# K's blocks projected before Q's, a second plain pair of tiles in V's phase, and ffn rounding spread over an iteration

## The chip, the cores and the metric

The kernel runs on one core of one Trainium2 chip. The metric is the device time of one execution in microseconds (us). The kernel before takes 2241.61 us (median of 3 runs, 2234.49 to 2244.3).

## The reference, cut to what matters

x is (8, 512, 1024), every weight 1024 x 1024. There are 16 heads of 64.

```python
q, k, v = proj(x, Wq), proj(x, Wk), proj(x, Wv)      # y = x @ W.T, split into heads
q = q * min(cond, 4)[:, None]                        # one factor for each batch
scores = q @ k.T / sqrt(64), causal                  # 512 x 512 for each head
out = softmax(scores) @ v ; y = out @ Wo.T
alpha = max(mean(|Wf|), 1e-5)
q_w = clip(round(Wf / alpha), -1, 1) * alpha         # ternary weights
q_y = clip(round(y / s), -128, 127) * s              # s = absmax of the row / 127
result = x + q_y @ q_w.T + bias
```

## The kernel before, in words

Every fp32 operand is held as a high part (rounded to fp32r) and a low part (the remainder), and each product is three passes: low by high, high by low, high by high. ScalarE (ACT) writes the high part, VectorE (DVE) or GpSimd (POOL) subtracts it to give the low part. The order of the instructions on each engine is written out by hand. There are three phases.

**V's phase.** The 32 token tiles of 128 are taken as 16 pairs. The first pair is computed plainly (`v_plain`, L788, 96 matmuls of 128x512 into the four banks of `s_ps` and `proj_ps`). The other 15 go by a Strassen-Winograd scheme of seven half-size products (`v_product`, L803, 7 x 12 = 84 matmuls), which needs sums of blocks of Wv (`wv_sums`, L720, on DVE, then `ws_high`, L730, on ACT and `ws_low`, L736, on DVE) and sums of blocks of x (`xv_sums`, L773, on POOL). Results go through `v_high` (L875) and `v_low` (L884) into the two halves of `v_out`, each stored by `store_v` (L699) before it is used again. In the same phase the ffn weight is made ternary, one slice in each of eight iterations (`wf_ternary`, L919, three DVE operations in a chain, written at the end of the iteration), and the first x of the next phase is loaded (`load_x`, L342).

**Attention.** 4 groups of 4 heads by 8 batches are 32 steps. A step overlaps `old` (the previous batch) with `now`. In it TensorE (PE) does, for `now`, four projections into `proj_ps` in the order of `groups` (L152): block 0 of Q, block 0 of K, block 1 of Q, block 1 of K, each 8 slices of 3 matmuls (L174). A block is two heads. `J(gi, k)` in the step is slice k of projection gi, `S(u)` the scores of unit u (4 heads by 4 query tiles, 16 units), `T(u)` the transposes of its probabilities, `PV(h)` the product with V. The step of `now` reaches its own S(0) after J(2,5), and units 6 to 15, so S(8) too, come in the next step, where the batch is called `old`.

When a projection is ready, ACT writes its high parts (`evac_hi`, L194) and DVE its low parts (`evac_lo`, L212), two heads each. In the programs of ACT and DVE this is V(0) to V(2), and V(3) is the first thing of the next step. High and low parts of a head lie in opposite halves of the partitions, and the scores need K with its halves exchanged as well, `k_sw`. This copy is made by two DMAs on SP's queue:

```python
def swap_k(sp, it, blk):
    sp.wait_ge(proj_lo_done, it * NEV + EVAC[2 * blk + 1])
```

The first head of each block waits for it (`if u % (2 * QT) == 0: pe.wait_ge(k_swapped[h // 2], ...)`, L235), so S(0) waits for the exchange of K's block 0 and S(8) for that of block 1. SP's queue in a step is, in order: exchange of block 1 of `old`, `load_x` of the next batch, `load_v` 0 and 1, `store_o` 0 of `old` (L336), exchange of block 0 of `now`, `load_v` 2 and 3, `store_o` 1 of `old`. `store_o` 1 waits for `o_add` of head 3 (`OA(3)`, L333 on DVE). Q's evacuation takes a factor that `batch_scale` (L367) computes on DVE for the next batch, after Q's block 1 has been evacuated, behind V(2). One unit runs S on PE, mask and row minimum on DVE (L253), exponential on ACT (L260), reciprocal on DVE (L266), scaling on POOL (L272), T on PE (L282), high part on ACT (L296), low part `L(u)` on DVE (L303). T(u) waits for L(u - 2), whose bank it takes.

**The end.** The output projection (L508) and the ternary product (L579) run over 32 token tiles.

Of the kernel before, what the change touches and what calls it, by code (L numbers as in the profile page):

```python
# [11 lines left out]
P = 128  # L12
# [24 lines left out]
def adaln_ffn_kernel(nc, x, xT, cond, wq, wk, wv, wo, wf, bias, out):  # L37
# [4 lines left out]
    with ExitStack() as ctx:  # L42
# [83 lines left out]
        w_in = [sem(f"w{n}_in") for n in "qk"]  # L126
# [25 lines left out]
        groups = [("q", 0), ("k", 0), ("q", 1), ("k", 1)]  # L152
# [5 lines left out]
        def project(pe, it, g, gi, k):  # L158
            kind, n = groups[gi]
            bank = proj_ps[gi % 2]  # L160
            w = "qkv".index(kind)
# [64 lines left out]
        def swap_k(sp, it, blk):  # L226
            sp.wait_ge(proj_lo_done, it * NEV + EVAC[2 * blk + 1])
            heads = slice(2 * blk, 2 * blk + 2)
            sp.dma_start(k_sw[0:DH, heads, :].bitcast(F32), k_st[DH:P, heads, :].bitcast(F32)).then_inc(k_swapped[blk], 16)  # L229
            sp.dma_start(k_sw[DH:P, heads, :].bitcast(F32), k_st[0:DH, heads, :].bitcast(F32)).then_inc(k_swapped[blk], 16)  # L230

        def scores(pe, it, u):
            h, qt = divmod(u, QT)
            n = it * UNITS + u
            if u % (2 * QT) == 0:  # L235
                pe.wait_ge(k_swapped[h // 2], (it + 1) * 32)
            if due(count := n - 1):
                pe.wait_ge(max_done, count)
# [128 lines left out]
        def batch_scale(dve, it, b):  # L367
# [15 lines left out]
        def load_w(sp, g):  # L383
            if due(count := 4 * g):
                sp.wait_ge(wqk_lo_done, count)
            for n in range(2):
                sp.dma_start(w_raw[n][:, :, :], (wq, wk)[n][bass.ds(g, 1), :, :, :]
                             .rearrange("a p k e -> p (a k) e")).then_inc(w_in[n], 16)

        def split_w_qk(eng, it, g, gi, low):  # L390

            kind, blk = groups[gi]
            w = "qkv".index(kind)
# [5 lines left out]
            else:  # L399
                eng.wait_ge(w_in[w], (g + 1) * 16)  # L400
                if isinstance(it, int) and it < 0:
                    eng.wait_ge(v_product_done, V_LAST + (1 if kind == "q" else 2))
# [229 lines left out]
        V_LAST = 7 * (PAIRS - 2)  # L632
# [4 lines left out]
        B_PLAIN = [[T2, T1], [T3, T4]]  # L637
# [12 lines left out]
        xv_sum_done = sem("xv_sum_done")  # L650
        v_plain_done = sem("v_plain_done")
# [23 lines left out]
        def plain_bank(j, i):  # L675
            return (s_ps, proj_ps)[j][i]

        def load_xv(sp, n):
            if n == 2:
                sp.wait_ge(xv_lo_done, 4)  # L680
            elif n > 2:
                sp.wait_ge(xv_lo_done, 4 + 7 * (n - 2))
# [16 lines left out]
        def store_v(sp, n, q):  # L699
            j, i = V_RESULT_PLAIN[q] if n == 0 else V_RESULT[q][:2]  # L700
# [29 lines left out]
        def ws_high(act, c):  # L730
            act.wait_ge(wv_sum_done, WV_SUM_COUNT[c])
            if c == A21_PLAIN:
                act.wait_ge(v_plain_done, 4)
# [9 lines left out]
        def xv_split_plain(eng, i, j, low):  # L743
            c = B_PLAIN[i][j]
            n = 2 * i + j
            if low:
                eng.wait_ge(xv_hi_done, n + 1)
                eng.tensor_tensor(xv[:, c, 1, :], xv_quad(0, i, j), xv[:, c, 0, :].bitcast(F32),
                                  ALU.subtract).then_inc(xv_lo_done, 1)
            else:  # L750
                eng.wait_ge(xv_first_in[i], 32)
                eng.activation(xv[:, c, 0, :], xv_quad(0, i, j), ACT.Copy).then_inc(xv_hi_done, 1)

        def xv_split(eng, n, c, low):
            if n >= PAIRS:
                return
            count = 4 + 7 * (n - 1) + c
# [7 lines left out]
            if n > 1:  # L765
                eng.wait_ge(v_product_done, 7 * (n - 2) + c + 1)
            elif c == T2:
                eng.wait_ge(v_plain_done, 4)
            if c >= T2:
                eng.wait_ge(xv_sum_done, 4 * (n - 1) + {T1: 1, T3: 2, T2: 3, T4: 4}[c])  # L770
            eng.activation(xv[:, c, 0, :], xv_quad(n, *XV_PLACE[c]), ACT.Copy).then_inc(xv_hi_done, 1)

        def xv_sums(pool, n):  # L773
# [3 lines left out]
            base, done = 4 + 7 * (n - 1), 4 * (n - 1)  # L777
# [9 lines left out]

        def v_plain(pe):  # L788
            for k in range(KT):
# [3 lines left out]
                ks = slice(k % CH * P, (k % CH + 1) * P)  # L793
                for j in range(2):
                    c = B_PLAIN[k // CH][j]
                    for i, a in enumerate((A11, A21_PLAIN) if k < CH else (A12, A22)):
                        for m, (xp, wp) in enumerate(((1, 0), (0, 1), (0, 0))):
                            mm = pe.matmul(plain_bank(j, i)[:, :], xv[:, c, xp, ks], wv_view(a, wp)[:, k % CH, :],
                                           start=(k == 0 and m == 0), stop=(k == KT - 1 and m == 2))
                        if k == KT - 1:  # L800
                            mm.then_inc(v_plain_done, 1)

        def v_product(pe, n, c):  # L803
            done = 4 * (n - 1)
            pe.wait_ge(xv_lo_done, 4 + 7 * (n - 1) + c + 1)
            if n == 1 and c in ws_lo_done:
                pe.wait_ge(ws_lo_done[c], 1)
            if c == A11:
                bank = bank_x[n % 2]
                if due(count := done - 4):  # L810
                    pe.wait_ge(v_sum_done, count)
            elif c == S4:
                bank = bank_w
                if due(count := done - 1):
                    pe.wait_ge(v_sum_done, count)
            elif c == A12:
                bank = bank_z
                if due(done):
# [21 lines left out]
        def v_copy(act, n, which):  # L840

            c, bank = [(A11, bank_x[n % 2]), (S2, bank_x[n % 2]), (S1, bank_z), (A22, bank_z)][which]
            act.wait_ge(v_product_done, 7 * (n - 1) + c + 1)
            if n > 1:
# [3 lines left out]
        def v_sum(dve, n, q):  # L848
            place = V_RESULT[q][2]
            if q == 0:  # L850
                bank = bank_z
                dve.wait_ge(v_product_done, 7 * (n - 1) + A12 + 1)
                dve.wait_ge(v_copy_done, 4 * (n - 1) + 1)
            elif q == 1:
                bank = bank_x[n % 2]
                dve.wait_ge(v_product_done, 7 * (n - 1) + S3 + 1)
                dve.wait_ge(v_ur_done, n)
            elif q == 2:
                bank = bank_w
# [11 lines left out]
        def v_source(n, q):  # L871
            src = plain_bank(*V_RESULT_PLAIN[q])[:, :] if n == 0 else v_tmp[:, V_RESULT[q][2], :]
            return src.rearrange("p (h d) -> p h d", d=DH)

        def v_high(act, n, q):  # L875
            if n == 0:
                act.wait_ge(v_plain_done, q + 1)
            else:
                act.wait_ge(v_sum_done, 4 * (n - 1) + q + 1)
# [12 lines left out]
        WF_ABS_FROM, WF_FROM = 2, 6  # L892
# [26 lines left out]
        def wf_ternary(dve, k):  # L919
            raw = wf_tmp[k % 2]  # L920
            dve.wait_ge(wf_in[k % 2], ((KT + k) // 2 + 1) * 16)
            if k >= 2:
                dve.wait_ge(wf_stored[k % 2], k // 2 * 16)
            dve.tensor_scalar(raw, raw, alpha[:, 1:2], MAGIC, ALU.mult, ALU.add).then_inc(wf_chain, 1)
            dve.wait_ge(wf_chain, 4 + 2 * k)
            dve.tensor_scalar(raw, raw, MAGIC, 1.0, ALU.subtract, ALU.min).then_inc(wf_chain, 1)
            dve.wait_ge(wf_chain, 5 + 2 * k)
            dve.tensor_scalar(wf_out[k % 2], raw, -1.0, None, ALU.max).then_inc(wf_q_done, 1)
# [9 lines left out]
        def v_sp(sp):  # L938
# [10 lines left out]
            for n in range(1, PAIRS):  # L949
# [4 lines left out]
                if n == 1:  # L954
# [13 lines left out]
                if n == WF_FROM + KT:  # L968
                    for slot in wf_stored:
                        sp.wait_ge(slot, KT // 2 * 16)  # L970
                    load_x(sp, 0, 0)

        def v_pe(pe):
            v_plain(pe)
            for n in range(1, PAIRS):
# [10 lines left out]
        def v_act(act):  # L986
            load_wv(act, 0)
            for i, (k0, k1) in enumerate(V_PIECES):
                if i == 0:
                    xv_split_plain(act, 0, 0, False)  # L990
                    xv_split_plain(act, 0, 1, False)
                if i == 2:
                    xv_split_plain(act, 1, 0, False)
                    xv_split_plain(act, 1, 1, False)
# [9 lines left out]
            xv_split(act, 1, T2, False)  # L1004
            xv_split(act, 1, T1, False)
            ws_high(act, S3)
            xv_split(act, 1, T3, False)
            xv_split(act, 1, T4, False)
            for q in range(4):
                v_high(act, 0, q)  # L1010
            for n in range(1, PAIRS):
# [638 lines left out]
```

## Time and profile before

| | |
|---|---|
| median of 3 runs | 2241.61 us |
| the profiled execution's own time | 2243.83 us |
| its span | 2241.8 us |
| mean granted TensorE clock | 0.975 |
| PE busy | 2033.3 us, 91% |
| DVE busy | 1422.6 us, 63% |
| ACT busy | 1119.2 us, 50% |
| POOL busy | 898.7 us, 40% |

The page of the profile divides the span into the busy time of the engines, the chain of work that ended last, and groups of instructions with the idle time ahead of them. A group's idle time is put down to what ended it. Answers of the trace used below are: who waited for whom, the instructions in order of time, and the busy time and granted clock of a stretch. V's phase runs to 341.6 us, attention to about 1760, and the end from there.

### The profile page before, as it was taken

To read this page: it belongs to the slowest core of one execution; us is meant where nothing else is said; L and a number is where in the kernel's file an instruction comes from. 1 tells how busy PE (TensorE), PEld (TensorE's weight loads), DVE (VectorE), ACT (ScalarE), POOL (GpSimd) and SP (SyncE) were. 2 spreads that over 40 slices of the span, in tenths; PEclk is the share of its full clock that TensorE was granted. 3 is DMA by queue.
4 is the path that set the end of the run, shared out by engine and by line. 5 is a ranking of instruction groups with operands and counts; after the bars stand their busy time and mean duration, and the time that the engine had idled before them with its cause. 6 is when DMAs were issued, how large, how long until landed. Compare 5 with 4: busy or idle time off the path is not lost.

```text
span 2241.8 us, 34702 instructions
## 1 busy us (share of the span) xinstructions
PE 2033.3 (91%) x10031; PEld 1640.5 (73%) x10062; DVE 1422.6 (63%) x3284; ACT 1119.2 (50%) x2504; POOL 898.7 (40%) x821
## 2 busy tenths in 40 slices
PE   6999998898989898898989888898988899999998
PEld 4778886776777777777767777777776677777776
DVE  7657775666667666667666667666666655445544
ACT  4454454666657666666666666666666300000000
POOL 2443333434334433434443343344334444444442
PEclk9999999999999999999999999999999999999999
DMA  5766644323343433343343334334235423333332
GB/s 150 239 221 211 209 178 148 104 90 119 117 134 94 131 103 98 103 163 105 95 131 103 98 103 165 104 94 140 94 98 158 134 95 102 112 112 95 102 112 75
DMA packets 200980, 282.42 MB, mean 126 GB/s; under 512 B 11216, under 2 KB 146384, under 8 KB 199760
## 3 DMA queue, kind: packets, MB, share of 16 engines
q1 hardware_dynamic: 200384, 281.07, 39.3%
q8 instruction: 33, 0.54, 0.1%
q10 hardware_dynamic: 528, 0.52, 0.1%
q14 instruction: 35, 0.29, 0.0%
HBM read 178.79 MB, written 69.21 MB: 111 GB/s over the span
## 4 chain that ended last, share of the span: by engine, by line
PE 69%; DMA 12%; DVE 9%; issue 4%; ACT 4%; SPq 2%; DVEq 0%; ACTq 0%
PE proj_ps L174 20%; DMA k_sw<-k_st 11%; PE s_ps L508 8%; PE proj_ps L508 7%; PE t_ps L835 7%; PE o_ps L316 7%; PE o_ps L835 5%; PE o_ps L579 5%; PE t_ps L282 4%; DVE k_st L223 4%; PE s_ps L241 3%; PE s_ps L242 2%; SPq L229 1%; DVE parts L364 1%; ACT pt_hi L296 1%
## 5 line engine op out<-in xcount | busy, mean ns | idle before, releaser
L174 PE MATMUL proj_ps<-parts 128*128 128x512 f32 x3072 | 858.3, 414 | 0.0
L272 POOL TENSOR_TENSOR prob<-prob,row_inv 128x128 f32<-128x128 f32 (+3 forms) x512 | 386.1, 754 | 846.3 <-DVE row_inv L266 843.9
L174 PEld LDWEIGHTS proj_ps<-parts 128*128 128x128 f32 x3072 | 550.1, 193 | 98.6
L260 ACT ACTIVATE prob<-prob,row_min 128x128 f32<-128x128 f32 (+3 forms) x512 | 287.2, 561 | 160.0 <-DVE row_min L253 155.5
L253 DVE CUSTOM_DVE_ANT_0 prob<-s_ps,mask 128x128 f32<-128x128 f32 (+3 forms) x512 | 248.3, 485 | 119.4 <-PE s_ps L242 54.9
L296 ACT ACTIVATE pt_hi<-t_ps 128x128 fp32r<-128x128 f32 (+3 forms) x512 | 221.9, 433 | 194.4 <-PE t_ps L282 189.1
L282 PE MATMUL t_ps<-ident,prob 128*128 128x128 f32 x1280 | 229.4, 277 | 52.8 <-DVE pt_lo L303 50.4
L303 DVE TENSOR_TENSOR pt_lo<-t_ps,pt_hi 128x128 fp32r<-128x128 f32 (+3 forms) x512 | 249.5, 487 | 31.0 <-ACT pt_hi L296 20.7
L241 PE MATMUL s_ps<-k_sw,q_st 128*128 128x128 f32 (+3 forms) x512 | 164.7, 322 | 114.9 <-DMA k_sw<-k_st 114.8
L564 ACT ACTIVATE yt_q<-t_ps 128x1024 bf16<-128x1024 bf16 x32 | 32.8, 1024 | 426.6 <-PE t_ps L557 426.6
L241 PEld LDWEIGHTS s_ps<-k_sw,q_st 128*128 128x128 f32 x512 | 96.8, 189 | 160.6 <-issue 108.9
L282 PEld LDWEIGHTS t_ps<-ident,prob 128*128 128x128 f32 x1280 | 152.5, 141 | 77.2 <-DVE pt_lo L303 46.9
L364 POOL TENSOR_TENSOR parts<-x_raw,parts 128x512 fp32r<-128x512 f32 x128 | 194.6, 1521 | 16.0 <-ACT parts L358 16.0
L333 DVE TENSOR_TENSOR o_sum<-o_ps,o_low 64x512 f32<-64x512 f32 x128 | 87.5, 683 | 172.4 <-ACT o_low L325 172.3
L508 PE MATMUL proj_ps<-parts,o_parts 128*128 128x512 f32 x768 | 188.2, 400 | 4.0 <-POOL o_parts L486 4.0
L508 PE MATMUL s_ps<-parts,o_parts 128*128 128x512 f32 x768 | 185.1, 396 | 0.0
L316 PE MATMUL o_ps<-pt_lo,v_st 128*128 128x512 f32 (+3 forms) x512 | 171.7, 345 | 2.6 <-DVE pt_lo L303 2.6
L508 PEld LDWEIGHTS proj_ps<-parts,o_parts 128*128 128x128 f32 x768 | 143.9, 190 | 35.1 <-POOL o_parts L486 4.2
L242 PE MATMUL s_ps<-k_st,q_st 128*128 128x128 f32 (+3 forms) x512 | 166.1, 324 | 0.0
L508 PEld LDWEIGHTS s_ps<-parts,o_parts 128*128 128x128 f32 x768 | 142.8, 188 | 30.6
L316 PE MATMUL o_ps<-pt_hi,v_st 128*128 128x512 f32 (+3 forms) x512 | 157.5, 343 | 0.0
L266 DVE RECIPROCAL row_inv<-row_sum 128x1 f32<-128x1 f32 x512 | 82.3, 161 | 102.0 <-ACT prob L260 98.7
(106 smaller groups left out, 2968.3 us busy)
## 6 DMA issues: line engine op xcount, KB each, us to landing
x_raw<-xT SPq DMA_DIRECT2D x128, 512.0 KB, 5.5
v_scratch<-v_out SPq DMA_DIRECT2D x64, 512.0 KB, 3.3
k_sw<-k_st SPq DMA_DIRECT2D x128, 256.0 KB, 3.7
v_st<-v_scratch SPq DMA_DIRECT2D x128, 256.0 KB, 2.7
oT_scratch<-o_sum SPq DMA_DIRECT2D x64, 256.0 KB, 2.1
x_raw<-oT_scratch SPq DMA_DIRECT2D x32, 512.0 KB, 4.8
x_tile<-x SPq DMA_DIRECT2D x32, 512.0 KB, 5.4
out<-res SPq DMA_DIRECT2D x32, 512.0 KB, 3.2
```

The costliest lines, as they stand in the source:

```text
L174: mm = pe.matmul(out, l, r, start=(k == 0 and i == 0), stop=(k == KT - 1 and i == 2))
L241: pe.matmul(s_ps[u % 2][:, 0:w], q, k_sw[:, h, 0:w], start=True, stop=False)
L253: dve.tensor_tensor_reduce(prob[:, u % 4, 0:w], s_ps[u % 2][:, 0:w], mask[:, S - w:S], 1.0, -MASKED, ALU.add, ALU.min, row_min[:, u % 4:u ...
L260: act.activation(prob[:, u % 4, 0:w], prob[:, u % 4, 0:w], ACT.Exp, bias=row_min[:, u % 4:u % 4 + 1], scale=-1.0, accum_out=row_sum[:, u % ...
L272: pool.tensor_tensor(prob[:, u % 4, 0:w], prob[:, u % 4, 0:w], row_inv[:, u % 4:u % 4 + 1].broadcast_to([P, w]), ALU.mult).then_inc(norm_d ...
L282: mm = pe.transpose(t_ps[u % 2][:, kb * P:(kb + 1) * P], prob[:, u % 4, kb * P:(kb + 1) * P], ident[:, :])
L296: act.activation(pt_view(pt_hi[h % 2], qt), t_ps[u % 2][:, 0:(qt + 1) * P] .rearrange("p (k q) -> p k q", q=P), ACT.Copy).then_inc(pt_hi_d ...
L303: dve.tensor_tensor(pt_view(pt_lo[h % 2], qt), t_ps[u % 2][:, 0:(qt + 1) * P] .rearrange("p (k q) -> p k q", q=P), pt_view(pt_hi[h % 2], q ...
L316: mm = pe.matmul(o_ps[h % 2][:, q0:S], v, part[h % 2][:, kb, q0:S], start=(kb == 0 and part is pt_lo), stop=(kb == QT - 1 and part is pt_hi))
L364: eng.tensor_tensor(x_lo[:, k, :], x_raw[:, k, :], x_hi[:, k, :].bitcast(F32), ALU.subtract).then_inc(x_lo_done[k % 2], 1)
L508: mm = pe.matmul(y_ps[p][half][:, :], a[p][:, o], b[k][:, w], start=(k == 0 and i == 0), stop=(k == KT - 1 and i == 2))
L835: mm = pe.matmul(bank[:, :], xv[:, c, xp, ks], wv_view(c, wp)[:, k, :], start=(k == 0 and m == 0 and c not in (S2, S3)), stop=(k == CH - 1 ...
```

## The change

Three parts. **Groups:** the order becomes K 0, Q 0, K 1, Q 1. The exchange of a block of K waits for K's evacuation (V(0), V(2)), which is one projection earlier; PE gets a wait for Q's evacuation at S(0) and S(8). On SP the exchange of `now`'s block 0 moves ahead of `load_v` 1 and `store_o` 0. `batch_scale` moves from behind V(2) to behind V(3), where Q's block 1 is evacuated now. The weights' buffers, loads and splits change places accordingly. **V's phase:** the second pair is plain as well, into the banks of `o_ps` and `t_ps`; fourteen pairs are left for the seven products. **ffn:** the three operations of the rounding are issued at three places of an iteration, the whole of that work runs one iteration later (from 7 instead of 6), and `load_x` waits for its last store at the start of the last iteration.

```diff
-        groups = [("q", 0), ("k", 0), ("q", 1), ("k", 1)]
+        groups = [("k", 0), ("q", 0), ("k", 1), ("q", 1)]
@@ swap_k
-            sp.wait_ge(proj_lo_done, it * NEV + EVAC[2 * blk + 1])
+            sp.wait_ge(proj_lo_done, it * NEV + EVAC[2 * blk])
@@ scores
                 pe.wait_ge(k_swapped[h // 2], (it + 1) * 32)
+                pe.wait_ge(proj_lo_done, it * NEV + EVAC[h // 2 * 2 + 1])
@@ batch_scale
-                if due(count := (it - 1) * NEV + EVAC[2]):
+                if due(count := (it - 1) * NEV + EVAC[3]):
@@ dve_step
             if old:
                 evac_lo(dve, o, 3)
+                if now:
+                    batch_scale(dve, n, now[2])
...
             V(2)
-            if nxt:
-                batch_scale(dve, *nxt)
@@ sp_step
             if now and old:
                 load_v(sp, *now, 0)
+            if now:
+                swap_k(sp, now[0], 0)
+            if now and old:
                 load_v(sp, *now, 1)
...
                 store_o(sp, *old, 0)
-            if now:
-                swap_k(sp, now[0], 0)
@@ V's phase
+        PLAIN = 2
-        B_PLAIN = [[T2, T1], [T3, T4]]
+        B_PLAIN = [[[T2, T1], [T3, T4]], [[B11, B21], [B22, T2]]]
+        PLAIN_BANKS = [s_ps + proj_ps, [bank_x[0], bank_w, bank_z, bank_x[1]]]
@@ v_plain, behind the first pair
+            for j in range(2):
+                pe.wait_ge(xv_lo_done, 4 + 2 * j + 2)
+                for i in range(2):
+                    for k in range(KT):
+                        mm = v_plain_slice(pe, 1, j, i, k)
+                    mm.then_inc(v_plain_done, 1)
@@ v_act, behind the splits of Wv
-            xv_split(act, 1, B11, False)
-            xv_split(act, 1, B22, False)
-            xv_split(act, 1, B21, False)
+            xv_split_plain(act, 1, 0, 0, False)
+            xv_split_plain(act, 1, 1, 0, False)
+            xv_split_plain(act, 1, 0, 1, False)
+            xv_split_plain(act, 1, 1, 1, False)
+            for q in range(4):
+                v_high(act, 0, q)
             ws_high(act, S4)
             ws_high(act, S2)
             ws_high(act, S1)
+            xv_split(act, 2, B11, False)
+            xv_split(act, 2, B22, False)
+            for q in range(2):
+                v_high(act, 1, q)
+            xv_split(act, 2, B21, False)
...
@@ v_dve
+                if n == WF_FROM:
+                    wf_scale(dve)
+                wf_ternary(dve, n - WF_FROM, 0)
...
                 v_low(dve, n, 0)
+                wf_ternary(dve, n - WF_FROM, 1)
...
                 xv_split(dve, n + 1, T1, True)
+                wf_ternary(dve, n - WF_FROM, 2)
...
-                if WF_FROM <= n < WF_FROM + KT:
-                    wf_ternary(dve, n - WF_FROM)
@@ v_sp
+                if n == PAIRS - 1:
+                    for slot in wf_stored:
+                        sp.wait_ge(slot, KT // 2 * 16)
+                    load_x(sp, 0, 0)
                 for q in range(4):
                     store_v(sp, n, q)
...
-                if n == WF_FROM + KT:
-                    for slot in wf_stored:
-                        sp.wait_ge(slot, KT // 2 * 16)
-                    load_x(sp, 0, 0)
```

## Rows read from the trace of the kernel before

**Rows 1.** The page: shares of the chain that ended last, by line.
```profile
PE proj_ps L174 20%; DMA k_sw<-k_st 11%; PE s_ps L508 8%; PE proj_ps L508 7%; PE t_ps L835 7%; PE o_ps L316 7%; PE o_ps L835 5%; PE o_ps L579 5%; PE t_ps L282 4%; DVE k_st L223 4%; PE s_ps L241 3%; PE s_ps L242 2%; SPq L229 1%; DVE parts L364 1%; ACT pt_hi L296 1%
```

**Rows 2.** Who waited for whom: us in total, times, longest.
```profile
PE s_ps L241 <- DMA k_sw<-k_st: 114.8, 63, 6.3
...
PE t_ps L282 <- DVE pt_lo L303: 50.4, 37, 1.7
```

**Rows 3.** Busy us and granted clock (PEclk, DMA share, GB/s last) of five stretches.
```profile
34.68:71.56 36.88, 24.05 (x85) 18.90 (x84) 27.57 (x26) 18.43 (x24) 7.48 (x5) 0.77 0.30 100
...
71.56:90.60 19.04, 19.04 (x85) 15.77 (x84) 11.00 (x15) 8.15 (x14) 7.25 (x5) 1.00 0.90 314
...
406.19:1716.63 1310.44, 1158.62 (x6000) 966.99 (x6000) 869.60 (x2442) 856.64 (x2052) 535.68 (x601) 0.97 0.36 115
...
1127.57:1150.51 22.94, 21.52 (x106) 18.03 (x107) 13.01 (x38) 12.38 (x30) 6.40 (x9) 0.93 0.45 148
...
1215.37:1236.72 21.35, 19.96 (x106) 16.79 (x107) 13.02 (x38) 12.37 (x30) 6.39 (x9) 1.00 0.48 158
```

**Rows 4.** PE in order of time, V's opening: start, us, instruction, idle before.
```profile
43.03 7.19 PE L835 MATMUL t_ps<-wv_first,xv 128*128 128x512 f32 x23 [5.47 <-DVE wv_first L738]
...
57.81 5.46 PE L835 MATMUL o_ps<-wv_first,xv 128*128 128x512 f32 x12 [7.36 <-ACT v_tmp L846]
```

**Rows 5.** DVE and ACT in order of time, V's opening.
```profile
36.32 2.29 DVE L728 TENSOR_TENSOR wv_raw<-wv_raw 128x2048 f32<-128x2048 f32 x1
...
38.65 3.71 ACT L734 ACTIVATE wv_first<-wv_raw 128x2048 fp32r<-128x2048 f32 x2 [14.22 <-DVE wv_raw L728]
...
55.28 0.60 ACT L882 ACTIVATE v_out<-proj_ps 128x512 fp32r<-128x512 f32 x1 [6.27 <-DMA v_scratch<-v_out]
```

**Rows 6.** PE in order of time, one step: S(0), T(4), S(8), the next S(0).
```profile
1062.76 0.33 PE L241 MATMUL s_ps<-k_sw,q_st 128*128 128x128 f32 x1 [1.31 <-DMA k_sw<-k_st]
...
1079.75 0.33 PE L282 MATMUL t_ps<-ident,prob 128*128 128x128 f32 x1 [1.27 <-DVE pt_lo L303]
...
1083.68 0.32 PE L241 MATMUL s_ps<-k_sw,q_st 128*128 128x128 f32 x1 [2.21 <-DMA k_sw<-k_st]
...
1106.62 0.32 PE L241 MATMUL s_ps<-k_sw,q_st 128*128 128x128 f32 x1 [1.44 <-DMA k_sw<-k_st]
```

**Rows 7.** DVE in order of time, the same step: V(2), batch_scale, OA(3), V(3), L(3).
```profile
1067.44 1.53 DVE L219 SCALAR_TENSOR_TENSOR q_st<-proj_ps,q_scale,q_st 64x512 fp32r<-64x512 f32 x2 [0.34 <-ACT q_st L204]
1069.01 0.15 DVE L374 TENSOR_SCALAR q_scale<-cond_bc 128x1 f32<-128x1 f32 x1
...
1075.69 0.68 DVE L333 TENSOR_TENSOR o_sum<-o_ps,o_low 64x512 f32<-64x512 f32 x1 [0.46 <-ACT o_low L325]
...
1077.70 1.41 DVE L223 TENSOR_TENSOR k_st<-proj_ps,k_st 64x512 fp32r<-64x512 f32 x2
...
1080.93 0.68 DVE L303 TENSOR_TENSOR pt_lo<-t_ps,pt_hi 128x512 fp32r<-128x512 f32 x1
```

**Rows 8.** SP's queue in order of time, the same step: store_o 1, exchange of block 1.
```profile
1076.45 0.36 SPq L340 DMA_DIRECT2D oT_scratch<-o_sum  x1
...
1079.65 0.59 SPq L230 DMA_DIRECT2D k_sw<-k_st  x1
```

**Rows 9.** Time from issue to landing: the exchanges (tile k_sw), and the page's DMA issues.
```profile
DMA to landing us min/median/max: 3.0/3.7/7.6
...
oT_scratch<-o_sum SPq DMA_DIRECT2D x64, 256.0 KB, 2.1
...
wf_scratch<-x_raw SPq DMA_DIRECT2D x8, 256.0 KB, 2.3
```

**Rows 10.** From V's phase into attention: SP, ACT, and a piece of the chain.
```profile
326.87 2.20 SPq L348 DMA_DIRECT2D x_raw<-xT  x4
...
338.05 0.58 ACT L846 ACTIVATE v_tmp<-t_ps 128x512 f32<-128x512 f32 x1
...
355.34 7.60 DMA k_sw<-k_st
```

More of the change, by code:

```diff
@@ L786, in xv_sums, with v_plain_slice @@
             pool.tensor_tensor(b21, b21, b22, ALU.subtract).then_inc(xv_sum_done, 1)
+        def v_plain_slice(pe, p, j, i, k):
+            c, a = B_PLAIN[p][k // CH][j], (A11, A21_PLAIN, A12, A22)[2 * (k // CH) + i]
+            ks = slice(k % CH * P, (k % CH + 1) * P)
+            for m, (xp, wp) in enumerate(((1, 0), (0, 1), (0, 0))):
+                mm = pe.matmul(PLAIN_BANKS[p][2 * j + i][:, :], xv[:, c, xp, ks], wv_view(a, wp)[:, k % CH, :],
+                               start=(k == 0 and m == 0), stop=(k == KT - 1 and m == 2))
+            return mm
         def v_plain(pe):
@@ L792, in v_plain @@
                     pe.wait_ge(xv_lo_done, 2 * (k // CH) + 2)
-                ks = slice(k % CH * P, (k % CH + 1) * P)
                 for j in range(2):
[L795 to L799, printed above, removed]
+                    for i in range(2):
+                        mm = v_plain_slice(pe, 0, j, i, k)
                         if k == KT - 1:
                             mm.then_inc(v_plain_done, 1)
+                if k == CH - 1:
+                    mm.then_inc(v_half_done, 1)
+            for j in range(2):
+                pe.wait_ge(xv_lo_done, 4 + 2 * j + 2)
+                for i in range(2):
+                    for k in range(KT):
+                        mm = v_plain_slice(pe, 1, j, i, k)
+                    mm.then_inc(v_plain_done, 1)
         def v_product(pe, n, c):
-            done = 4 * (n - 1)
-            pe.wait_ge(xv_lo_done, 4 + 7 * (n - 1) + c + 1)
-            if n == 1 and c in ws_lo_done:
+            done = v_first(n)
+            pe.wait_ge(xv_lo_done, xv_count(n) + c + 1)
+            if n == PLAIN and c in ws_lo_done:
                 pe.wait_ge(ws_lo_done[c], 1)
@@ L967, in v_sp @@
                         load_wf(sp, KT + k + 2)
[L968 to L971 removed]
         def v_pe(pe):
             v_plain(pe)
[L975 removed]
+            for n in range(PLAIN, PAIRS):
                 v_product(pe, n, A11)
@@ L1003, in v_act @@
             ws_high(act, S1)
-            xv_split(act, 1, T2, False)
-            xv_split(act, 1, T1, False)
-            ws_high(act, S3)
[L1007 to L1011, printed above, removed]
+            xv_split(act, 2, B11, False)
[3 more added lines that the diff above has]
+            xv_split(act, 2, B21, False)
+            xv_split(act, 2, T2, False)
+            v_high(act, 1, 2)
+            xv_split(act, 2, T1, False)
+            ws_high(act, S3)
+            v_high(act, 1, 3)
+            xv_split(act, 2, T3, False)
+            xv_split(act, 2, T4, False)
+            for n in range(PLAIN, PAIRS):
                 v_copy(act, n, V_TMP_A)
@@ L1088, in v_dve @@
                 v_low(dve, n, 3)
-                if n == WF_FROM:
-                    wf_scale(dve)
-                if WF_FROM <= n < WF_FROM + KT:
-                    wf_ternary(dve, n - WF_FROM)
         def v_pool(pool):
-            xv_sums(pool, 1)
-            for n in range(1, PAIRS):
+            xv_sums(pool, PLAIN)
+            for n in range(PLAIN, PAIRS):
                 xv_sums(pool, n + 1)
```

182 lines of the change are left out of this document (107 added, 75 removed).

## The prediction

> **What bounds the kernel now.** I read the page's chain first. Behind the projections (20%) its largest item is no engine but a transfer: the exchange of K's halves, 11% of the span [rows 1]. The list of waits says what of that PE feels: S(0) and S(8) wait for it 63 times, 114.8 us in all [rows 2]. PE's only other large wait in attention is for the low parts of the probabilities, 50.4 us. Then the instructions of one step in order of time: S(8) at 1083.68 waits 2.21 us, S(0) at 1106.62 waits 1.44 [rows 6]. Of the 63, one is the first S(0) (6.34 us by its row, 6.3 here); the 31 others at S(0) are 1.31 to 1.44 us, say 1.39, together 43.1; what is left, 114.8 - 6.3 - 43.1 = 65.4 us, is 31 waits at S(8), 2.11 each.
>
> The stretches show a second cost. S(8) to S(0) takes 21.35 us at a granted clock of 1.00 and 22.94 us at 0.93, the same work [rows 3]: after the waits at T(4) (1.27 us) and S(8) PE runs for a while at 1.2 instead of 2.4 GHz. 22 of the 31 such stretches are slow ones, so 22 x 1.57 = 34.5 us hang on PE's idling there. After S(0)'s single 1.4 us the clock does not fall.
>
> In V's phase PE is full (19.04 busy of 19.04 us for a pair [rows 3]) but for its opening: pair 1 takes from 34.68 to 71.56, 36.88 us, PE busy 24.05 at a clock of 0.77. It waits 5.47 us for the sums of Wv and 7.36 us for ACT, which sits 6.27 us waiting for a store of `v_out` before it may copy a bank [rows 4, 5].
>
> **V's opening.** The new plain pair is 96 matmuls where the old product had 84. A product's matmul is 19.04/84 = 0.2267 us at the full clock, so the pair costs 96 x 0.2267 = 21.76 us in place of 36.88: 15.1 us less, if nothing waits. Its splits of x come where the old ones came, ahead of the sums of Wv. The sums and splits of Wv now have the pair as cover: the sums end at 38.6 or sooner [rows 5], ACT is held by `v_high` of pair 0 (two of them wait for a store) until 41 to 44, then three `ws_high` of 1.85 us (half of 3.71 [rows 5]) and three `ws_low` on DVE of 2.3 us, a sum's time [rows 5], end at 49.5 to 52.5, and PE reaches the first product at 56.5. ACT must then pass two splits, `v_high` 1/2 and 1/3, a split, the last `ws_high` and two more splits, some 6.5 us, before the copy that frees pair 2's third accumulation, which PE reaches 8.2 us later: a slack of 1.7 us; DVE's first sum has under 1 us. Bounds for what is late next: 0 and 3 us. I take 0.3, since both slacks are above zero; without this cover the old stalls of 5.47 and 7.36 us come back. **-14.8 us.** The other 14 pairs do not change.
>
> **ffn rounding.** Three DVE operations of 0.7 us leave the end of an iteration. PE waits for nothing of theirs there (full at 1.00), and at the new places the splits of x run an iteration ahead: 0, bounds -0.5 and +1. But one thing moves with it: the last store of that work is now issued at about 327 and `load_x`, behind it on SP, waits for its landing, 2.3 us [rows 9], where it was issued at 326.87 [rows 10]. ACT's eight splits of x stand ahead of the copy at 338.05, which PE's last product waits for with no slack (it starts 0.15 us late already). x_high waited for no DMA before, so the cover is somewhere between 0 and 2.4 us: +0 to +2.4, I take **+1.3**.
>
> **S(0).** K 0 is evacuated at V(0), a projection of 24 matmuls and more before V(1), so at least 5.4 us sooner, and its exchange is issued then. On SP it stands behind `load_v` 0, which waits for PV(0), done before V(0); `load_v` 1 and `store_o` 0 behind it wait for PV(1) and later work, so nothing queued there is held. It lands 3.7 us on, well before S(0). The new wait is for Q 0's low parts at V(1), where the exchange began until now; an exchange takes 0.5 + 3.7 us, of which PE waits 1.4, so PE arrives 2.8 us after V(1). Behind the wait stand only T(13) and PV(2), ready by then. DVE's row minimum follows S(0) at once and its reciprocal before it ends 0.3 us ahead. **31 x 1.39 = -43.1 us.** The first S(0): four loads of x go ahead of the exchange on SP at 350.4, so it is issued at about 352.5 instead of 355.3 and its 7.6 us [rows 10] still show: **-2.5**.
>
> **S(8).** K 1 is evacuated at V(2), but the exchange stands on SP behind `store_o` 1, which waits for OA(3). Counted from S(0) at 1062.76 [rows 6]: OA(3) ends 13.6; the store takes SP 0.4, the exchange's halves 0.5 each, so the second is issued at 14.6 instead of 16.9 [rows 7, 8]; with 3.7 to 3.9 us it lands at 18.3 to 18.5. PE reaches S(8) at 20.92 - 2.21 = 18.7. On DVE, V(3) is Q's now: 1.53 instead of 1.41, and `batch_scale` 0.15 with its wait [rows 7], so L(2), T(4) and S(8) come 0.25 later, at 19.0; the low part L(3), which T(5) right behind S(8) needs, ends at 18.85 + 0.25 = 19.1, about when T(5) would go. V(2) is cheaper by as much, but DVE idles behind it anyway, so I give nothing for that. The store before the exchange lands 2.1 us after its issue [rows 9] and may delay it by up to 0.9. So of 2.11 us between 0.25 and 1.3 stay; by the nearest numbers (DVE's 0.25 and a little of the other) I take 0.35. **31 x 1.76 = -54.5 us.** `load_x` behind the exchange still waits for the last split of x, as before.
>
> **Clock.** With 1.5 to 1.9 us of idling at T(4) and S(8) in place of 3.4, more than after S(0) and less than now, the fall should go in most steps. Bounds 0 and -34.5; I take **-28**.
>
> Sum: -14.8 + 1.3 - 2.5 - 43.1 - 54.5 - 28 = -141.6 us, against the profiled execution's 2243.8: 2102. That execution is 2.2 us over the median of the runs shown, less than their spread of 9.8, so I leave it. As a check, attention's period is 1310.44/30 = 43.7 us [rows 3], and would be 43.7 - 1.39 - 1.76 - 0.9 = 39.6, with PE busy some 37.9 of it.
>
> **Rivals.**
>
> (a) The clock stays. PE's small waits go on (T(4) alone 1.27 us), and the stretches from S(8) may stay slow: 2102 + 28 = 2130. For it: 22 of 31 stretches fall now; against it: no stretch falls after S(0), whose wait is nearly as long as what will be left at S(8). The Trainium skill ("TensorE: Matmul & The Clock Gate", section "A second HAM failure mode: psum-queue depth-cycling") says that frequent micro-idles between groups of matmuls are enough to make the clock swing between its two levels; by that rule this rival would be the forecast.
>
> (b) The exchange of block 1 is as late as ever. If it and the store ahead of it share the engines fully, it lands 2.1 us later, at 20.5, against 20.9 now: S(8) gains 0.4 instead of 1.76, and the clock falls as before. 2102 + 31 x 1.36 + 28 = 2172. For it: two transfers on one queue within 0.5 us. Against it: the store's bytes are half of the exchange's, and it has landed by 15.8.
>
> (c) Slower. The same place, with the price that the trace shows when an exchange runs beside big loads: 7.6 us [rows 9, 10]. Behind the moved exchange comes `load_x`, four loads. Landing at 14.6 + 7.6 = 22.2 makes S(8) 1.3 us later than now, which eats S(0)'s 1.39; the clock would fall in the 9 other stretches too (+14), V's phase keeps its 13.5 and the first step 2.5: about 2239. Each further microsecond costs 31: from 8.1 us of landing on the kernel is over 0.5% slower, and at 8.5 it takes 2239 + 31 x 0.9 = 2267. Against it: `load_x` waits for the last split of x and is issued at 1082.4, 4.8 us after the moved exchange. The Trainium skill ("DMA: Bandwidth & Descriptors", section "Issuing engines are not separate DMA queues") says that all DMAs interleave on the same 16 engines, which is what makes this rival possible and says nothing of its size.
>
> (d) The change doesn't do what it says in attention, since Q's evacuation, now last, takes the place of the exchange. At S(0) it is done 2.8 us ahead; V(3) ends at 1079.1, 2.4 us ahead of PE at S(8) [rows 6, 7]. Nothing speaks for it; with only V's part left it would take about 2230.
>
> **Chances.** Forecast 0.64, (a) 0.18, (b) 0.10, (c) 0.03, (d) 0.02, and 0.03 for something under 2080. The forecast's own range is 2083 (all of the clock back and no residue: -14.8 - 2.5 - 43.1 - 65.4 - 34.5 = -160, and nothing lost at V's end) to 2120. With (a) and part of (b), and 1.0 us more at S(8) in a case between, the range is 2080 to 2150. 0.5% is 11 us, about what a measurement of this kernel tells from no change. Faster than that: all but (c) and a share of (d), 0.95; the same 0.03; slower 0.02.
>
> **What would show it.** PE's wait for `k_sw` under 25 us in total, and none at S(0) but the first; S(0) to S(0) near 39.6 us; the granted clock of S(8) to S(0) at 1.00; plain pair 1 at 34.7 to 56.5 with no wait over 0.5 us behind it; the last product of V's phase 1 to 2 us behind the one before. A sum of waits for `k_sw` over 60 us is rival (b); a clock of 0.93 with short waits is (a). The forecast is wrong as a whole if PE's waits for `pt_lo` (50.4 us now) grow past 80: then DVE, not the exchange, set S(8).

## The result

The changed kernel takes 2085.72 us (median of 4 runs, 2083.93 to 2087.4) against 2241.44 before: a ratio of 0.9309 (95% interval 0.9287 to 0.9332), 156 us less. It lies in the range given; the forecast was 2102.

The page of the changed kernel, its span, busy times and the chain by line (for [rows 1]); its own time is 2085.09 us at a mean clock of 0.994:

```profile
span 2083.3 us, 34749 instructions
...
PE 1991.5 (96%) x10074; PEld 1617.8 (78%) x10074; DVE 1416.1 (68%) x3277; ACT 1114.4 (53%) x2497; POOL 888.4 (43%) x816
...
PE proj_ps L174 24%; PE proj_ps L509 8%; PE s_ps L509 8%; PE o_ps L317 6%; PE o_ps L580 5%; PE t_ps L870 5%; PE t_ps L283 5%; PE o_ps L870 3%; PE s_ps L243 2%; PE s_ps L242 2%; DVE q_st L219 2%; ACT parts L359 2%; DVE prob L254 2%; DVE parts L365 1%; ACT prob L261 1%
```

The exchange, 11% of the chain before, is no longer among its lines. What PE still waits for most, from the list of waits (for [rows 2]; us, waits, the longest):

```profile
PE t_ps L283 <- DVE pt_lo L304: 50.8, 35, 2.8
```

and who waited for the tile `k_sw`, from the view of that tile:

```profile
  PE s_ps L242: 1.6, 2
```

Besides these two waits (0.45 us at one S(8), 1.14 us at one S(0)) the first S(0) waits 4.85 us. The list puts that down to "issue", but it is the exchange too: it was issued at 342.79, took 10.1 us to land, and S(0) starts at 352.97. So 114.8 us of waiting for the exchange, 6.3 of them at the first S(0), have become 6.5. The wait for `pt_lo` has not grown.

Five stretches (for [rows 3]): the new plain pair, the first pair of seven products, all 31 periods from S(0) to S(0), and the two parts of one step, S(0) to S(8) and S(8) to S(0):

```profile
34.00:55.76 21.76, 21.76 (x98) 18.03 (x96) 12.72 (x12) 8.62 (x9) 4.20 (x3) 1.00 0.56 193
55.76:74.80 19.04, 19.04 (x86) 15.77 (x84) 15.94 (x18) 11.81 (x20) 9.61 (x6) 1.00 0.43 139
...
352.97:1556.34 1203.37, 1151.61 (x6176) 973.49 (x6177) 893.59 (x2517) 881.59 (x2114) 552.17 (x619) 1.00 0.42 129
...
1130.57:1149.34 18.77, 17.33 (x96) 14.40 (x94) 14.54 (x40) 15.86 (x38) 10.58 (x11) 1.00 0.24 70
1149.34:1169.13 19.79, 19.79 (x107) 16.96 (x108) 13.82 (x43) 12.33 (x31) 7.18 (x10) 1.00 0.54 172
```

A period, from one S(0) to the next, is 1203.37/31 = 38.82 us where it was (1716.63 - 363.08)/31 = 43.66; the first and last S(0) before stood at 363.08 and 1716.63. From S(8) to S(0) PE is busy without a gap, at the full clock. Between the two profiled executions the span's 158.5 us come from: 8.6 until attention's first matmul (341.62 to 332.99), 1.5 from there to the first S(0), 150.2 in the 31 periods, and 1.8 back in the end.

PE, DVE and SP in order of time in that step (for [rows 6 to 8]): T(4), S(8) and the next S(0); OA(3), V(3), batch_scale, L(3); store_o 1, the exchange of block 1 behind it, load_x, the exchange of block 0.

```profile
1147.57 0.33 PE L283 MATMUL t_ps<-ident,prob 128*128 128x128 f32 x1 [1.41 <-DVE pt_lo L304]
...
1149.33 0.32 PE L242 MATMUL s_ps<-k_sw,q_st 128*128 128x128 f32 x1
...
1169.13 0.22 PE L242 MATMUL s_ps<-k_sw,q_st 128*128 128x128 f32 x1
```

```profile
1143.09 0.69 DVE L334 TENSOR_TENSOR o_sum<-o_ps,o_low 64x512 f32<-64x512 f32 x1 [0.45 <-ACT o_low L326]
...
1145.11 1.53 DVE L219 SCALAR_TENSOR_TENSOR q_st<-proj_ps,q_scale,q_st 64x512 fp32r<-64x512 f32 x2
1146.78 0.15 DVE L375 TENSOR_SCALAR q_scale<-cond_bc 128x1 f32 x1
...
1148.75 0.68 DVE L304 TENSOR_TENSOR pt_lo<-t_ps,pt_hi 128x512 fp32r<-128x512 f32 x1
```

```profile
1143.99 0.37 SPq L341 DMA_DIRECT2D oT_scratch<-o_sum  x1
1144.89 0.47 SPq L229 DMA_DIRECT2D k_sw<-k_st  x1
1145.41 0.59 SPq L230 DMA_DIRECT2D k_sw<-k_st  x1
1150.21 1.90 SPq L349 DMA_DIRECT2D x_raw<-xT  x4
...
1156.79 0.48 SPq L229 DMA_DIRECT2D k_sw<-k_st  x1
```

Two places gave less than was forecast. PE's last product of V's phase, then the first S(0) (for [rows 10]; the columns are start, us, instruction, idle before it):

```profile
328.67 4.48 PE L870 MATMUL t_ps<-wv_last,xv 128*128 128x512 f32 x12 [2.84 <-ACT v_tmp L881]
...
352.97 0.45 PE L242 MATMUL s_ps<-k_sw,q_st 128*128 128x128 f32 x1 [4.85 <-issue]
```

and ACT ahead of that product, where the splits of x wait for their loads, which stand on SP behind the landing of the last ffn store:

```profile
322.43 2.43 ACT L359 ACTIVATE parts<-x_raw 128x512 fp32r<-128x512 f32 x4 [1.40 <-DMA x_raw<-xT]
325.66 2.38 ACT L359 ACTIVATE parts<-x_raw 128x512 fp32r<-128x512 f32 x4 [0.80 <-DMA x_raw<-xT]
327.94 0.58 ACT L881 ACTIVATE v_tmp<-t_ps 128x512 f32<-128x512 f32 x1
```

### The profile page after: what moved, and what is told of

Same layout as the page of the kernel before. It is cut to its first block, busy times and chain, and to the rows that moved or that the text cites. A ratio compares the mean times of both kernels' runs of the same rounds, so it can differ in the third digit from the quotient of the medians.

```text
span 2083.3 us, 34749 instructions
## 1 busy us (share of the span) xinstructions
PE 1991.5 (96%) x10074; PEld 1617.8 (78%) x10074; DVE 1416.1 (68%) x3277; ACT 1114.4 (53%) x2497; POOL 888.4 (43%) x816
## 4 chain that ended last, share of the span: by engine, by line
PE 72%; DVE 10%; issue 6%; ACT 6%; DMA 3%; POOL 1%; DVEq 0%; SPq 0%; ACTq 0%; POOLq 0%
PE proj_ps L174 24%; PE proj_ps L509 8%; PE s_ps L509 8%; PE o_ps L317 6%; PE o_ps L580 5%; PE t_ps L870 5%; PE t_ps L283 5%; PE o_ps L870 3%; PE s_ps L243 2%; PE s_ps L242 2%; DVE q_st L219 2%; ACT parts L359 2%; DVE prob L254 2%; DVE parts L365 1%; ACT prob L261 1%
## 5 line engine op out<-in xcount | busy, mean ns | idle before, releaser
L174 PE MATMUL proj_ps<-parts 128*128 128x512 f32 x3072 | 840.9, 408 | 0.0
L174 PEld LDWEIGHTS proj_ps<-parts 128*128 128x128 f32 x3072 | 540.6, 190 | 95.8
L283 PE MATMUL t_ps<-ident,prob 128*128 128x128 f32 x1280 | 228.2, 277 | 53.1 <-DVE pt_lo L304 50.8
L242 PE MATMUL s_ps<-k_sw,q_st 128*128 128x128 f32 (+3 forms) x512 | 160.3, 313 | 7.5 <-issue 5.0
L317 PE MATMUL o_ps<-pt_lo,v_st 128*128 128x512 f32 (+3 forms) x512 | 161.2, 326 | 2.7 <-DVE pt_lo L304 2.7
L359 ACT ACTIVATE parts<-x_raw 128x512 fp32r<-128x512 f32 x256 | 146.0, 618 | 3.1 <-DMA x_raw<-xT 2.2
L317 PE MATMUL o_ps<-pt_hi,v_st 128*128 128x512 f32 (+3 forms) x512 | 147.0, 324 | 0.0
```

The source lines that it names most:

```text
L174: mm = pe.matmul(out, l, r, start=(k == 0 and i == 0), stop=(k == KT - 1 and i == 2))
L242: pe.matmul(s_ps[u % 2][:, 0:w], q, k_sw[:, h, 0:w], start=True, stop=False)
L283: mm = pe.transpose(t_ps[u % 2][:, kb * P:(kb + 1) * P], prob[:, u % 4, kb * P:(kb + 1) * P], ident[:, :])
L317: mm = pe.matmul(o_ps[h % 2][:, q0:S], v, part[h % 2][:, kb, q0:S], start=(kb == 0 and part is pt_lo), stop=(kb == QT - 1 and part is pt_hi))
```

## The experiments

All ratios are to the kernel before, timed beside it on the same chip.

**The change in two.** `groups_only` is the kernel before with the edits of `groups`, `swap_k`, `scores`, `batch_scale` and SP's order; `v_only` is the changed kernel with these undone.

> The kernel before with the attention part of the change alone (order K 0, Q 0, K 1, Q 1, the exchange's place on SP, batch_scale's place). Theory: the step of the changed kernel, 38.82 us instead of 43.66, comes wholly from this part: 31 x 4.84 = 150 us and 1.5 us at the first S(0), so 2090 us. Rival 1: the terms as I forecast them (1.39 + 1.76 a step and 28 of the clock): 2113. Rival 2: part of the step's gain needs V's phase (it starts attention in another state): above 2100 as well, with the clock below 0.99.

Measured: 2094.37 us, 0.9329 (0.9315 to 0.9343). Its mean period is 38.74 us. The theory holds for the step: the attention part alone gives 150 us, at a step that owes nothing to V's phase. Its 1.5 us at the first S(0) did not come: S(0) starts at 363.70 us, against 363.08 before, after a wait of 7.16.

> The kernel before with V's phase and the ffn rounding of the change, attention as it was. Theory: pair 1 takes 21.76 us instead of 36.88 (-15.1), V's end loses 2.8 us of waiting and 1.6 us of slow clock, and three small waits in the middle lose 2.3: -8.4, so 2233 us, with the step unchanged at 43.7. Rival (the late load of x shows only with the new order of the groups): -13, 2228.

Measured: 2232.68 us, 0.9949 (0.9935 to 0.9963), 11.5 us less. The interval, 8 to 15 us less, holds the theory's 8.4 and the rival's 13, so the trace has to tell. In order of time on PE: the last product has the same kind of wait ahead of it, 3.53 us; attention's first matmul starts at 335.59 us, 6.0 sooner than before and 2.6 later than in the changed kernel; and the first S(0) waits 2.70 us where it waited 6.34 before:

```profile
330.34 5.46 PE L869 MATMUL t_ps<-wv_last,xv 128*128 128x512 f32 x12 [3.53 <-ACT v_tmp L880]
335.59 9.71 PE L174 MATMUL proj_ps<-parts 128*128 128x512 f32 x40
...
353.90 0.44 PE L241 MATMUL s_ps<-k_sw,q_st 128*128 128x128 f32 x1 [2.70 <-DMA k_sw<-k_st]
```

So the late load of x is V's own, against the rival. The first S(0) comes 9.2 us sooner than before, near the theory's 8.4, but only 6.0 of them are there at attention's start; the other 3.2 come with the shorter wait, which the theory did not have. The mean period is 43.43 us, with 21 slow stretches from S(8) instead of 22.

**One block at a time.**

```diff
# block0_only (on the kernel before)
-        groups = [("q", 0), ("k", 0), ("q", 1), ("k", 1)]
+        groups = [("k", 0), ("q", 0), ("q", 1), ("k", 1)]
# block1_only (on the kernel before, with batch_scale behind V(3))
+        groups = [("q", 0), ("k", 0), ("k", 1), ("q", 1)]
```

Each exchange waits for its own block, and `scores` for the other operand where that is evacuated later.

> The kernel before with the order K 0, Q 0, Q 1, K 1: only block 0 is exchanged a projection sooner. Theory (the clock falls because of the waits at T(4) and S(8) together): S(0)'s wait of 1.39 us goes 31 times, S(8) keeps its 2.1 us and the stretches after it stay at a granted clock of 0.93: 2241 - 43 - 2 = 2197 us. Rival (the clock falls with the idle time of a step as a whole): the clock comes back too, 34 us more: 2162.

Measured: 2171.23 us, 0.967 (0.9655 to 0.9685). That is between the two and nearer to the rival (2162) than to the theory (2197). The waits are as the theory has them, 64.7 us over 31 at S(8), and none at S(0) but the first (6.2 us):

```profile
PE s_ps L242 <- DMA k_sw<-k_st: 64.7, 31, 2.4
```

but only 9 of the 31 stretches from S(8) to S(0) are slow, not 22 as before. The same stretch at both clocks:

```profile
425.46:446.79 21.33, 21.32 (x107) 18.25 (x107) 12.73 (x37) 11.51 (x29) 5.57 (x8) 0.92 0.48 157
467.76:487.56 19.80, 19.80 (x107) 16.97 (x107) 12.75 (x37) 11.52 (x29) 5.55 (x8) 1.00 0.51 170
```

Taking away S(0)'s wait, 20 us earlier in the step, prevented 13 of the clock's falls, worth 13 x 1.5 = 20 us. My reason for the falls, "after the waits at T(4) and S(8)", is half of it. How a wait so much earlier bears on them, no run shows.

> The kernel before with the order Q 0, K 0, K 1, Q 1: only block 1 is exchanged a projection sooner, and batch_scale moves. Theory: S(8)'s 2.11 us go and with them the clock's fall (34.5 us), S(0) keeps its 1.39: 2241 - 66 - 34 = 2140 us, granted clock 1.00 from S(8) to S(0). Rival (PE's small waits keep the clock low): 2175 us at a clock of 0.97.

Measured: 2144.67 us, 0.955 (0.9536 to 0.9565), near the theory. S(0) waits 1.3 to 1.6 us each time but the first, as in this row of PE in order of time:

```profile
688.32 0.33 PE L242 MATMUL s_ps<-k_sw,q_st 128*128 128x128 f32 x1 [1.30 <-DMA k_sw<-k_st]
```

Yet no stretch is slow; 400 us from the middle of attention, whose clock is the column of 1.00:

```profile
800.00:1200.00 400.00, 370.02 (x1981) 309.90 (x1980) 287.41 (x806) 283.78 (x678) 177.01 (x199) 1.00 0.39 123
```

The periods fall by 2.32 and 3.28 us, 174 us for both in 31 steps where the two together give 150: each alone brings back most of the clock (13 and 22 of the 22 falls), and it comes back once.

**What the queue's order is worth: rival (c).** `load_x` ahead of the exchange of block 1 in `sp_step`.

```diff
-            if old:
-                swap_k(sp, old[0], 1)
             if nxt:
                 load_x(sp, *nxt)
+            if old:
+                swap_k(sp, old[0], 1)
```

> The changed kernel with load_x ahead of the exchange of block 1 on SP, to price rival (c) of the prediction. The exchange is issued about 22 us after S(0) instead of 14.6 and runs beside four loads of 512 KB. Theory (transfers issued together share the engines): it lands 7 to 11 us after its issue, S(8) is 10 to 14 us later, 310 to 430 us in all, with the clock down in every step: 2400 to 2550 us. Rival (an exchange takes 3.7 us whatever runs beside it): S(8) is 6.5 us later, 2290 to 2330 us.

Measured: 2524.7 us, 1.1263 (1.1232 to 1.1293), at a mean clock of 0.914. The loads, the exchange, and PE at S(8), in one step:

```profile
1015.05 1.89 SPq L349 DMA_DIRECT2D x_raw<-xT  x4
1017.10 0.56 SPq L229 DMA_DIRECT2D k_sw<-k_st  x1
1017.70 0.61 SPq L230 DMA_DIRECT2D k_sw<-k_st  x1
```

```profile
1027.00 0.47 PE L242 MATMUL s_ps<-k_sw,q_st 128*128 128x128 f32 x1 [12.82 <-DMA k_sw<-k_st]
```

1027.0 - 1017.7 = 9.3 us from issue to use, where an exchange alone takes 3.7; over the 30 steps the second half lands 8.3 to 9.5 us after its issue. The theory holds, and rival (c)'s price is real. At S(8) its place is not in the changed kernel, where `load_x` is issued 4.8 us behind the exchange (1150.21 and 1145.41 above). But the same collision is there for block 0, whose exchange moved ahead of `load_v` 1. The view of the tile `k_sw` of the changed kernel:

```profile
DMA to landing us min/median/max: 3.1/3.7/13.2
```

In three steps, the first of each later group, this exchange is issued behind `load_x`, the loads of both weights and `load_v` 0, and lands after 10.4 to 13.2 us. S(0) comes late enough that PE waited for it only once, 1.14 us.

**V's end and the first step.**

```diff
# wf_store_early
                 for q in range(4):
                     store_v(sp, n, q)
+                    if q == 0 and WF_FROM <= n < WF_FROM + KT:
+                        store_wf(sp, n - WF_FROM)
...
-                    store_wf(sp, k)
# first_exchange: in the first step only, ahead of load_x
+            if now and not old:
+                swap_k(sp, now[0], 0)
...
-            if now:
+            if now and old:
                 swap_k(sp, now[0], 0)
```

> The changed kernel with the store of a rounded slice of the ffn weight issued behind the first of an iteration's four stores of V instead of behind the fourth. Theory: load_x no longer waits for that store's landing, PE's last product in V's phase loses its wait of 2.84 us and the slow clock behind it (1.6 us): -4.4, 2081 us. Rival (the loads of x themselves are the late ones, since they start after the fourth store of V either way): -1 or less.

Measured: 2082.88 us, 0.9289 (0.927 to 0.9307). `load_x` is issued 2.1 us sooner and PE's last product waits 0.4 us instead of 2.8, as the theory has it:

```profile
316.11 3.23 SPq L349 DMA_DIRECT2D x_raw<-xT  x4
```

In time the gain is 0.2% of the kernel, and its interval meets that of the changed kernel; the wait is shown, its 4 us are not. In the trace attention starts at 331.00 us. That is 2.0 sooner than in the changed kernel's profiled execution, which was a short one (see `first_exchange` below), and 4.9 to 6.3 sooner than in four others with its V's phase. The first S(0) gains less, 0.5 us against the changed kernel, since it now waits 6.39 us for the exchange instead of 4.85: the two edits of this section act on one path.

> The changed kernel with the exchange of block 0 ahead of load_x on SP in the first step only. Theory: the first S(0) waits 4.85 us because the exchange runs behind four loads of x; ahead of them it takes 3.7 us, the wait goes and with it the slow clock of some 3 us after it: -7 us, 2079. Rival (Q 0's evacuation is as late): -1 or less.

Measured: 2080.71 us, 0.9279 (0.926 to 0.9298). The wait at the first S(0) is gone, and the first step is 36.29 us long instead of 38.05. From attention's start to the first S(0) it is 15.0 us instead of 20.0, so with the step's 1.8 the size in the trace is the expected one; the interval overlaps with the changed kernel's by its edge.

This trace shows something more, since its V's phase is the changed kernel's, instruction for instruction. Yet attention starts at 335.89 us, not 332.99. PE waits 3.4 us for the sum of the ffn weight at 159 us in both, and behind that wait the clock was 1.00 in the changed kernel's profiled execution and 0.89 here:

```profile
158.00:190.00 32.00, 30.63 (x136) 25.41 (x137) 22.83 (x29) 14.31 (x27) 12.99 (x9) 1.00 0.65 203
...
158.00:190.00 32.00, 31.44 (x127) 25.86 (x128) 20.59 (x27) 12.93 (x24) 11.19 (x9) 0.89 0.58 186
```

It is 0.89 in `l2_first`, `l2_free` and `load_x_first` too, whose V's phase is also the same; attention starts at 336.4 to 337.3 there. So the profiled execution of the changed kernel was the lucky one of five: in the others V's phase ends 2.9 to 4.4 us later.

**The ffn rounding.** The three parts together at the end of an iteration again, in `v_dve`.

> The changed kernel with the three operations of the ffn rounding together at the end of an iteration again, at its new iterations. Theory (PE never waited for their place; what they set is when the last store, and behind it load_x, is issued): no other wait of PE in V's phase changes, the last rounding ends some 5 us later than in three parts, so load_x is issued 2 to 4 us later and V's end loses that: 2085 + 3 = 2088 us. Rival (three parts shorten waits in the middle of V's phase): three waits of PE of 0.6 to 1 us more in every iteration from 7 on, 2093 or more.

Measured: 2089.62 us, 0.9315 (0.9287 to 0.9344): no difference that the measurement tells. PE's waits in V's phase are the last product's, 3.7 us instead of 2.8, and 1.1 us at two others, so the rival's new waits are not there. `load_x` is issued 2.9 us later than in the changed kernel's profiled execution. But `first_exchange`, whose rounding is in three parts, has it as late. Its row of SP in order of time, behind that of `ffn_together`:

```profile
321.17 1.76 SPq L349 DMA_DIRECT2D x_raw<-xT  x4
...
321.05 1.76 SPq L349 DMA_DIRECT2D x_raw<-xT  x4
```

So the delay is not shown to come from the edit, and what the three places are worth, if anything, stays open.

**What is late next.** T(4) waits 1.41 us in each step for L(2), which stands behind V(3).

```diff
# l2_first, on DVE (and H(2) ahead of evac_hi on ACT)
+            L(2)
             if old:
                 evac_lo(dve, o, 3)
                 if now:
                     batch_scale(dve, n, now[2])
-            L(2)
# l2_free, besides: the exchange as soon as V(2) is done, ahead of store_o 1
-            if old:
+            if ending:
                 swap_k(sp, old[0], 1)
...
+            if now and not last:
+                swap_k(sp, now[0], 1)
             if old:
                 store_o(sp, *old, 1)
# l2_free_x6, besides (with wf_store_early and first_exchange):
# DVE's split of slice 6 from behind M(6) to behind L(4) and I(7)
```

> The changed kernel with the high and low parts of unit 2 (H(2) on ACT, L(2) on DVE) ahead of the evacuation V(3) instead of behind it, to price what is late now: T(4)'s wait for pt_lo, 1.41 us a step. Theory (DVE's order at the start of a step sets T(4), and V(3) has slack until S(8)): the wait goes, T(5)'s need of L(3) gives 0.2 back, 31 x 1.2 = 37 us less: 2086 - 37 = 2049 us. Rival (V(3) or the exchange becomes the last to arrive at S(8) at once, since its slack is no larger than what PE gains): S(8) waits for it and the kernel takes 2075 to 2086.

Measured: 2092.53 us, 0.9325 (0.9307 to 0.9344). My theory was wrong, and the rival's mechanism is right, though the time is above its 2086: T(4)'s wait went (10.7 us in all instead of 50.8) and the exchange took its place at once, 43.3 us over 29. In the profiled execution, the longest of its five at 2098.82 us, six stretches from S(8) are slow as well. The end of L(3) on DVE and S(8) on PE in one step:

```profile
1161.79 0.68 DVE L304 TENSOR_TENSOR pt_lo<-t_ps,pt_hi 128x512 fp32r<-128x512 f32 x1
```

```profile
1162.39 0.32 PE L242 MATMUL s_ps<-k_sw,q_st 128*128 128x128 f32 x1 [1.64 <-DMA k_sw<-k_st]
```

> l2_first with the exchange of block 1 issued ahead of store_o 1 as well, as soon as V(2) is done. In l2_first T(4)'s wait is gone, but S(8) waits 1.64 us for the exchange, which store_o 1 holds back, and L(3) ends just when T(5) starts. Theory (three things arrive at S(8) together, and DVE's own work from S(0) to L(3), 18.8 us, is the last of them): the wait for k_sw goes to nothing, T(5) waits for L(3) instead, S(0) to S(8) plus T(5)'s wait stays at 18.8, and the kernel takes 2078 to 2088 us. Rival (only the exchange was left): S(0) to S(8) falls to 17.3, 31 x 1.4 = 43 us less, 2043.

Measured: 2087.68 us, 0.931 (0.9281 to 0.9338). As the theory has it: of the waits for `k_sw` one of 0.2 us is left, and two waits for DVE stand in its place, at S(8) for the bank and at T(5) for L(3):

```profile
1149.71 0.33 PE L242 MATMUL s_ps<-k_sw,q_st 128*128 128x128 f32 x1 [0.58 <-DVE row_min L254]
...
1151.01 0.41 PE L283 MATMUL t_ps<-ident,prob 128*128 128x128 f32 x2 [0.86 <-DVE pt_lo L304]
```

> l2_free with DVE's split of x's slice 6 (0.86 us) moved from ahead of L(3) to behind L(4), and with wf_store_early and first_exchange. Theory (DVE's order up to L(3) is the bound): T(5) goes 0.7 to 0.9 us sooner in 31 steps, 22 to 28 us, and V's end and the first step give 5 and 5: 2048 us from 2085. Rival (the split is only moved in front of a later need, J(0,6) or load_x): nothing in the step, 2075.

Measured: 2063.97 us, 0.9204 (0.9177 to 0.9231), the fastest kernel of this study. The commonest period falls from 38.5 to 38.16 us, so the move gives 0.35 us a step, 11 in all, not 22 to 28: T(5) still waits 0.48 us for L(3). The rest is V's end and the first step (35.74 us), which three edits share; how much is each one's was not run with this order.

## Why the prediction was right, and where its sizes were off

The mechanism was right: the two exchanges were the wait, `groups_only` gives 150 of the 156 us, and the exchange of block 1 stays off the path by the queue's order that was worked out. The sum, -141.6, came out at -158.7 between the profiled executions, and the largest part of the difference is the term of S(8).

- **V's opening, -14.8.** 36.88 to 21.76 us [rows 3, 4], -15.1, with no wait behind it. Right. But later in V's phase, where I said nothing changes, PE has 0.60 and 0.95 us of waits for ACT and 0.7 more at the ffn weight's sum, 3.4 us instead of 2.7. Their cause was not tested. Behind that sum the clock fell in four of the five executions with this V's phase (`first_exchange` above) and not in the one compared here, so the 8.6 us that V's phase gave are 4.3 to 5.7 in the others. That part of the total is luck.
- **V's end, +1.3.** The mechanism was named; the size was 2.7 us more waiting and 1.6 us at the lower clock, +4.3, over my bound of 2.4. The store landed 4.1 us after its issue, not the median 2.3 [rows 9], and I had left out that a wait can lower the clock. `v_only` and `wf_store_early` show it.
- **S(0), -43.1.** One wait of the 31 is left, 1.14 us at the start of a group, and `block0_only` shows the waits go with this block alone. The prediction's reading of them was a little off: one of the 31 was 2.65 us, not 1.31 to 1.44, so those at S(0) are 44.4 us and those at S(8) 64.1, or 2.07 each. The first S(0), -2.5, gave -1.5: the exchange behind four loads took about 10 us, not 7.6 [rows 10]; `first_exchange` shows that. In `groups_only` this term gave nothing.
- **S(8), -54.5.** Here is the term that was mis-sized most among the waits: I left 0.35 us of residue a step, and S(0) to S(8) fell by 2.20 on average, all of the wait and a little: 68 us in place of 54.5. I gave nothing for the cheaper V(2), "since DVE idles behind it anyway". But what DVE idles for there is ACT's split of x, and ACT's V(2) is cheaper too (1.21 us instead of 1.39), so OA(3) ends 13.2 us after S(0) instead of 13.6, and V(3), now 0.27 dearer, starts 0.4 sooner [rows 7]. This is read from the traces; no run separates it.
- **Clock, -28.** One slow stretch in 31 instead of 22: -33. The bound of -34.5 was the right value. The reason given was too narrow (`block0_only`), which did no harm since both waits went. The three terms of the step make some 144 of its 150.2 us. The rest was in no term: without S(0)'s wait a stretch at the full clock is 19.8 us, not 21.35 - 1.39, and one stretch before took 25.45.
- **Rivals.** (a), the clock stays, is out. The Trainium skill ("TensorE: Matmul & The Clock Gate", section "A second HAM failure mode: psum-queue depth-cycling") describes a kernel in which frequent micro-idles between groups of matmuls make the clock swing. Here the swing is gone with one wait of 1.41 us a step; in `l2_first`, with one of 0.8 to 2.1 us at S(8) itself, 6 stretches are slow, four of them behind waits of 1.75 to 1.79 us. (b) is out: the exchange is issued 0.9 us behind the store, and in the 31 steps PE waits for it once, 0.45 us. (c) was priced too low, 7.6 against 8.3 to 9.5 us of landing; it doesn't occur at S(8), and at block 0's exchange it occurs three times behind enough slack. (d) is out, since `groups_only` gives 150 us. The sign that would have told of DVE as the bound, `pt_lo` past 80 us, is not there; yet `l2_free` shows that DVE is next, with 0.58 us at S(8) and 0.86 at T(5).

One step of the changed kernel, 702.52 to 743.6, takes 41.08 us: T(4) waits 2.64 us and the clock falls. The same step is 1.0 to 2.8 us longer than its neighbours in the six other runs that hold both parts of the change, other than `load_x_first`, where the steps vary too much to tell; `groups_only` and `v_only` have no such step. What causes it stays open. By their ratios `groups_only` and `v_only` together give 7.2% of the kernel and the changed kernel 6.9%; the difference, 0.3%, is no larger than the intervals taken together, so nothing has to be explained there.

## What to carry to other kernels

When a transfer sits between two stages, order the stages ahead of it so that its operand is made first, and put it on its queue ahead of anything large: 3.7 us becomes about 9 behind four loads. When two waits are removed, price the clock once for both, since each alone may bring it back. Before moving work off the late item, list what else arrives there: in this kernel four things (`pt_lo` at T(4), the exchange and a bank at S(8), L(3) at T(5) behind it) come due within about two microseconds, and removing the first, then the first two, gave nothing. And read a stretch that a change should not have touched in several traces before a few microseconds of it are put down to the change: V's phase ended up to 4.4 us apart in five executions of the same instructions.

## What the runs showed that I had not expected

The lower clock after S(8) goes with a wait 20 us earlier as well: with S(0)'s 1.39 us gone and S(8)'s 2.1 us kept, 9 of 31 stretches are slow instead of 22. The time of a transfer of 256 KB within SBUF went with what was issued in the 2 us before it: 3.7 us behind a 256 KB store, 8.3 to 9.5 behind four loads of 512 KB. And the clock after PE's wait of 3.4 us in V's phase was 1.00 in one profiled execution and 0.89 in four others of the same instructions.
